# Masked attention over 64 keys against one-hot fetching of six picked keys, in a three-stage perceiver block

## The reference

```
xn   = layernorm(x) * gamma + beta
h    = xn @ W1.T                                     # 128 features
pair = relu(h[i] - h[j] + b1); pair = relu(pair @ W2.T + b2)
sim  = pair @ W3.T + b3;  sim[i, i] = 0              # 64 x 64 numbers
top6 = the six largest of each row of sim            # int(64 * 0.1) = 6
q, k, v = split(xn @ Wqkv.T + bqkv)                  # 32 heads of 2 features
scores  = q . k / sqrt(2), -inf where j is not in top6
out     = softmax(scores) @ v @ Wout.T + bout;  x + out
```

## Time and profile before

| | us |
|---|---|
| median of three runs | 2090.74 (2090.61 to 2090.97) |
| the profiled execution | 2089.24 |
| its span, first to last instruction | 2087.9 |

### The profile page before, as it was taken

The page is one execution under the profiler, slowest core; times in us unless marked ns, Lnnn a source line. Parts: engine busy times, 40 slices in busy tenths (PEclk is TensorE's granted clock), DMA queues, the critical chain, the costliest instruction groups (busy, mean ns, idle before and its releaser), DMA issues. The chain is left out here.

```text
span 2087.9 us, 31319 instructions
## 1 busy us (share of the span) xinstructions
PE 1943.7 (93%) x10316; PEld 1638.9 (78%) x10316; DVE 1152.3 (55%) x2987; ACT 968.3 (46%) x1955; POOL 649.3 (31%) x738
## 2 busy tenths in 40 slices
PE   3999999999999999999999999999999998758869
PEld 3778888888888888888888888888888887532447
DVE  6565465545554554466546655664556445148743
ACT  4564454446555654455445544554445444118221
POOL 3224543222232232333333333334333321011310
PEclk9999999999999999999999999999999999879769
DMA  5675454434453544354435444544444343720020
GB/s 191 207 258 158 118 151 121 150 106 148 141 182 116 162 136 137 115 168 144 133 106 168 144 142 123 177 143 153 119 155 144 96 145 92 250 81 3 1 81 20
DMA packets 228080, 280.94 MB, mean 135 GB/s; under 512 B 63241, under 2 KB 133513, under 8 KB 227921
## 3 DMA queue, kind: packets, MB, share of 16 engines
q1 hardware_dynamic: 217424, 278.09, 42.5%
q10 hardware_dynamic: 8448, 0.43, 0.2%
q0 software_dynamic: 2048, 0.43, 0.1%
HBM read 239.10 MB, written 39.22 MB: 133 GB/s over the span
## 5 line engine op out<-in xcount | busy, mean ns | idle before, releaser
L505 PE MATMUL kx_ps<-ctxT_hi,wk_hi 128*128 128x400 f32 (+1 forms) x1024 | 367.1, 358 | 16.0 <-DVE ctxT_lo L295 14.7
L507 PE MATMUL kx_ps<-ctxT_lo,wk_hi 128*128 128x400 f32 (+1 forms) x1024 | 356.9, 349 | 0.0
L509 PE MATMUL kx_ps<-ctxT_hi,wk_lo 128*128 128x400 f32 (+1 forms) x1024 | 356.2, 348 | 0.0
L588 PE MATMUL u_ps<-ctxN_hi,pt_hi 128*128 128x512 f32 (+1 forms) x832 | 341.5, 410 | 6.7 <-DVE pt_lo L826 6.4
L589 PE MATMUL u_ps<-ctxN_lo,pt_hi 128*128 128x512 f32 (+1 forms) x832 | 330.9, 398 | 0.0
L590 PE MATMUL u_ps<-ctxN_hi,pt_lo 128*128 128x512 f32 (+1 forms) x832 | 329.1, 396 | 0.0
L826 DVE TENSOR_TENSOR pt_lo<-t_ps,pt_hi 128x512 fp32r<-128x512 f32 (+1 forms) x256 | 144.6, 586 | 250.6 <-ACT pt_hi L1106 250.6
L1075 ACT ACTIVATE kx_hi<-kx_ps 128x400 fp32r<-128x400 f32 (+1 forms) x256 | 128.8, 503 | 320.6 <-PE kx_ps L509 317.3
L1106 ACT ACTIVATE pt_hi<-t_ps 128x512 fp32r<-128x512 f32 (+1 forms) x256 | 125.5, 523 | 265.1 <-PE t_ps L573 265.1
L753 DVE TENSOR_TENSOR kx_lo<-kx_ps,kx_hi 128x400 fp32r<-128x400 f32 (+1 forms) x256 | 146.6, 573 | 184.1 <-ACT sq L1077 183.5
L808 DVE CUSTOM_DVE_ANT_0 prob<-sc_ps,rstd_bc 128x400 f32<-128x400 f32 (+2 forms) x256 | 136.4, 570 | 140.1 <-PE sc_ps L561 140.1
(11 more groups left out here) (253 smaller groups left out, 3643.1 us busy)
## 6 DMA issues: line engine op xcount, KB each, us to landing
rstd_bc<-scratch_rstd SPq DMA_DIRECT2D x64, 804.0 KB, 6.0
stage<-in_ctx_t SPq DMA_DIRECT2D x96, 267.0 KB, 4.2
stage<-in_ctx_n SPq DMA_DIRECT2D x96, 256.0 KB, 6.1
wk_hi<-scratch_wk_s SPq DMA_DIRECT2D x56, 256.0 KB, 3.2
wk_lo<-scratch_wk_s SPq DMA_DIRECT2D x56, 256.0 KB, 3.7
wv_hi<-scratch_wv_s SPq DMA_DIRECT2D x56, 256.0 KB, 4.9
wv_lo<-scratch_wv_s SPq DMA_DIRECT2D x56, 256.0 KB, 5.6
scratch_own_rows<-out_sb SPq DMA_DIRECT2D x32, 256.0 KB, 2.9
```

The costliest lines, as they stand in the source:

```text
L505: PE.matmul(kx_ps[:, j % 2, 0:w], wk_hi[:, g % 2, i, :], ctxT_hi[:, i, c0:c0 + w], start=(i == 0), stop=False)
L507: PE.matmul(kx_ps[:, j % 2, 0:w], wk_hi[:, g % 2, i, :], ctxT_lo[:, i, c0:c0 + w], start=False, stop=False)
L509: mm = PE.matmul(kx_ps[:, j % 2, 0:w], wk_lo[:, g % 2, i, :], ctxT_hi[:, i, c0:c0 + w], start=False, stop=(i == C - 1))
L588: PE.matmul(u_ps[:], pt_hi[0:w, t % 2, cols], ctxN_hi[0:w, y, :], start=(y == 0), stop=False)
```

## The change

Only stage 2 and its loads are changed. In place of all 64 scores, only the six picked keys are computed. DVE writes a 0/1 mask laid out by batch (`mask`, 128 x 4 x 128). PE turns it, and one product with a triangular matrix (`rankmat`) numbers the picked keys of each token 1 to 6 (unpicked ones get a number that no rank matches). For each rank t, DVE makes a one-hot matrix (`hot`) and PE multiplies it with keys and values side by side (`kv`), which fetches key and value of rank t for every token and head. The rest works on 6 x 128 numbers for each partition, where x = 4 pairs of batches x 32 heads.

The query, key and value products become one product of 192 columns for each 128 tokens, with the bias as a product with a row of ones, and stand behind the pair loop in PE's order. The doubling of yT, the value blocks, the key spreads and the masks go. Tail.load has 7 counted DMAs in place of 11; the projection weights come in one DMA with rows of 768 bytes.

```diff
@@ Tail.load
-        for h in range(2):
-            SP.dma_start(self.wq2[:, :, h, :], qkv[:, :, 0:64]).then_inc(d_in, 16)
-        for h in range(2):
-            SP.dma_start(self.wk2[:, :, h, :], qkv[:, :, 64:128]).then_inc(d_in, 16)
-        SP.dma_start(self.wv[:], qkv[:, :, 128:192]).then_inc(d_in, 16)
+        SP.dma_start(self.wqkv[:], dram["wqkvT"].rearrange("(c p) o -> p c o", p=P)).then_inc(d_in, 16)
+        SP.dma_start(self.bqkv[0:1, :], dram["bqkv"]).then_inc(d_in, 16)
...
-        SP.dma_start(self.blockmask[:], dram["blockmask"]).then_inc(d_in, 16)
-        SP.dma_start(self.halfmask[:], dram["halfmask"]).then_inc(d_in, 16)
+        SP.dma_start(self.rankmat[:], dram["rankmat"]).then_inc(d_in, 16)
@@ tensor(), behind the h product: the products L1787, L1791, L1797 go
@@ tensor(), behind the pair loop: weigh and mix go, and
+            PE.wait_ge(zeroed, 4)
+            for t in range(4):
+                out = s_ps[:, 1 + t // 2, 192 * (t % 2):192 * (t % 2) + 192]
+                for c in range(4):
+                    PE.matmul(out, yT[:, c, t * P:(t + 1) * P], wqkv[:, c, :], start=(c == 0), stop=False)
+                mm = PE.matmul(out, one_row[0:1, :], bqkv[0:1, :], start=False, stop=True)
+                if t % 2:
+                    mm.then_inc(qkv_done, 1)
+            PE.wait_ge(topk_step, 12)
+            PE.wait_ge(sim_moved, 8)
             for k in range(4):
+                mm = PE.transpose(sim_ps[:, k * P:(k + 1) * P], mask[:, k, :], ident[:])
+            mm.then_inc(mask_turned, 1)
+            PE.wait_ge(mask_moved, 1)
+            PE.wait_ge(w3_set, 3)
+            PE.matmul(v_ps[:], rankmat[:], maskT[:], start=True, stop=True).then_inc(ranked, 1)
...
+            for t in range(TOPK):
+                PE.wait_ge(hot_done, t + 1)
+                for k in range(4):
+                    mm = PE.matmul(gather_banks[t][:, k * P:(k + 1) * P], hot[:, t, k * P:(k + 1) * P], kv[:, k, :],
+                                   start=True, stop=True)
+                mm.then_inc(gathered, 1)
@@ vector(): the copies L1871, the value blocks L1888 and L1891, and weigh and mix go, and
+            for b2 in range(2):
+                hr = slice(64 * b2, 64 * b2 + 64)
+                V.tensor_scalar(mask[hr, :, hr], picked[hr, :, 0:64], BIG, 1.0, ALU.is_equal, ALU.mult).then_inc(topk_step, 1)
+            def one_hot(t):
+                V.tensor_scalar(hot[:, t, :], v_ps[:], t - 99.0, 1.0, ALU.is_equal, ALU.mult).then_inc(hot_done, 1)
+            def multiply(t):
+                V.wait_ge(gathered, t + 1)
+                V.tensor_tensor(prod[:, t, :, :], gather_banks[t].rearrange("p (x f) -> p x f", f=4)[:, :, 0:2],
+                                q_sb[:].rearrange("p k (h d) -> p (k h) d", d=2), ALU.mult).then_inc(multiplied, 1)
+            V.wait_ge(ranked, 1)
+            V.wait_ge(qkv_moved, 4)
+            one_hot(0)
+            one_hot(1)
+            for t in range(TOPK):
+                if t + 2 < TOPK:
+                    one_hot(t + 2)
+                multiply(t)
+            V.wait_ge(multiplied, TOPK)
+            V.tensor_tensor(sc[:], prod[:, :, :, 0], prod[:, :, :, 1], ALU.add).then_inc(s_step, 1)
+            V.wait_ge(s_step, 1)
+            V.tensor_reduce(mx[:], sc[:].rearrange("p t x -> p x t"), AX.X, ALU.max).then_inc(s_step, 1)
+            V.wait_ge(s_step, 2)
+            V.tensor_tensor(sc[:], sc[:], mx[:].unsqueeze(1).broadcast_to([P, TOPK, P]), ALU.subtract).then_inc(s_step, 1)
+            V.wait_ge(s_exp, 1)
+            V.tensor_tensor(prod[:, 0:4, :, :].rearrange("p t x d -> p (t x) d"),
+                            s_ps[:].rearrange("p t (x f) -> p (t x) f", f=4)[:, :, 2:4],
+                            prob[:, 0:4, :].rearrange("p t x -> p (t x)").unsqueeze(2).broadcast_to([P, 4 * P, 2]),
+                            ALU.mult).then_inc(s_step, 1)
+            V.tensor_tensor(prod[:, 4:6, :, :].rearrange("p t x d -> p (t x) d"),
+                            b_ps[:].rearrange("p t (x f) -> p (t x) f", f=4)[:, :, 2:4],
+                            prob[:, 4:6, :].rearrange("p t x -> p (t x)").unsqueeze(2).broadcast_to([P, 2 * P, 2]),
+                            ALU.mult).then_inc(s_step, 1)
+            V.tensor_reduce(sm[:], prob[:].rearrange("p t x -> p x t"), AX.X, ALU.add).then_inc(s_step, 1)
+            V.wait_ge(s_step, 6)
+            V.reciprocal(inv[:], sm[:]).then_inc(s_step, 1)
+            V.tensor_reduce(mixed_sb[:], prod[:].rearrange("p t x d -> p x d t"), AX.X, ALU.add).then_inc(s_step, 1)
+            V.wait_ge(s_step, 8)
+            V.tensor_tensor(ao[:].rearrange("p k (h d) -> p (k h) d", d=2), mixed_sb[:],
+                            inv[:].unsqueeze(2).broadcast_to([P, P, 2]), ALU.mult).then_inc(ao_done, 1)
@@ scalar(): behind hT and hTb, in place of the query and key moves
+            A.wait_ge(zeroed, 1)
             for b2 in range(2):
                 hr = slice(64 * b2, 64 * b2 + 64)
+                A.activation(w3b[hr, b2:b2 + 1], core.col("w3")[hr, :], ACTF.Copy).then_inc(w3_set, 1)
+            A.activation(rankmat[:], tail.rankmat[:], ACTF.Copy).then_inc(w3_set, 1)
@@ scalar(): behind the pair loop, in place of the exponentials and moves
+            for pair in range(2):
+                A.wait_ge(qkv_done, pair + 1)
+                src = s_ps[:, 1 + pair, 0:384].rearrange("p (k e) -> p k e", k=2)
+                A.activation(kv[:, 2 * pair:2 * pair + 2, :], src[:, :, 64:192], ACTF.Copy).then_inc(qkv_moved, 1)
+                A.activation(q_sb[:, 2 * pair:2 * pair + 2, :], src[:, :, 0:64], ACTF.Copy).then_inc(qkv_moved, 1)
+            A.wait_ge(mask_turned, 1)
+            A.activation(maskT[:], sim_ps[:], ACTF.Copy).then_inc(mask_moved, 1)
+            A.wait_ge(s_step, 3)
+            A.activation(prob[:], sc[:], ACTF.Exp, scale=2.0 ** -0.5).then_inc(s_exp, 1)
@@ gpsimd(): the four key spreads L2018 go; four memsets stand ahead of the additions L2028 and L2031
+            G.memset(mask[:], 0.0).then_inc(zeroed, 1)
+            G.memset(one_row[:], 1.0).then_inc(zeroed, 1)
```

More of the change, by code:

```diff
@@ L27 @@
 N_ROWS = 0
-for _name, _n in (("bout", 512), ("ffn_b2", 512), ("bv", 64), ("wq_scale", 1), ("wqx_scale", 1),
+for _name, _n in (("bout", 512), ("ffn_b2", 512), ("wq_scale", 1), ("wqx_scale", 1),
                   ("wk_scale", 1), ("wv_scale", 1), ("proj_w_scale", 1), ("proj_in_scale", 1), ("b3", 1)):
@@ L1763, in sparse_attention @@
+        maskT, hot = sb("maskT", [P, 512], F32R), sb("hot", [P, TOPK, 512])
+        prod = sb("prod_d", [P, TOPK, P, 2])
+        sc, prob = sb("sc_d", [P, TOPK, P]), sb("prob_d", [P, TOPK, P])
+        mx, sm, inv = sb("mx_d", [P, P]), sb("sm_d", [P, P]), sb("inv_d", [P, P])
+        mixed_sb, ao, aoT = sb("mixed_d", [P, P, 2]), sb("ao_d", [P, 4, 64]), sb("aoT_d", [64, 512])
         banks = [b_ps[:, 0, :], b_ps[:, 1, :]]
         d_in = tail.d_in
-        hqk_done, v_done, doubled = sem("hqk_done"), sem("v_done"), sem("y_doubled")
@@ L1784, in tensor @@
                 mm = PE.matmul(s_ps[:, 0, :], wh[:, c, :], yT[:, c, :], start=(c == 0), stop=(c == 3))
-            mm.then_inc(hqk_done, 1)
-            for c in range(4):
-                mm = PE.matmul(s_ps[:, 1, :], wq2[:, c, :, :].rearrange("p h e -> p (h e)"), yT[:, c, :],
-                               start=(c == 0), stop=(c == 3))
-            mm.then_inc(hqk_done, 1)
-            for c in range(4):
-                mm = PE.matmul(s_ps[:, 2, :], wk2[:, c, :, :].rearrange("p h e -> p (h e)"), yT[:, c, :],
-                               start=(c == 0), stop=(c == 3))
-            mm.then_inc(hqk_done, 1)
-            PE.wait_ge(doubled, 2)
-            for b in range(8):
-                for c in range(4):
-                    mm = PE.matmul(v_ps[:, b * 64:(b + 1) * 64], vx_in[:, c, b, :, :].rearrange("p h s -> p (h s)"),
-                                   wv[:, c, :], start=(c == 0), stop=(c == 3))
-            mm.then_inc(v_done, 1)
+            mm.then_inc(h_done, 1)
             def last_layer(group):
@@ L1867, in vector @@
         def vector():
-            V.wait_ge(d_in, 16 * 11)
-            V.wait_ge(feat.moved, 8)
-            for h in range(2):
-                V.tensor_copy(vx_in[:, :, :, h, :], yT[:].rearrange("p c (b s) -> p c b s", b=8)).then_inc(doubled, 1)
             def first_layer(unit):
@@ L1913, in vector @@
             V.wait_ge(topk_step, 10)
-            V.tensor_scalar(mask[:], picked[:, :, 0:64], BIG, -1.0e30, ALU.not_equal, ALU.mult).then_inc(topk_step, 1)
-            V.wait_ge(topk_step, 11)
-            def weigh(k):
-                V.wait_ge(s_done, k + 1)
-                after(V, s_less, k)
-                V.scalar_tensor_tensor(sc[:], s_ps[:].rearrange("p i (h j) -> p (i h) j", j=64), 2.0 ** -0.5,
-                                       mask[:, k, :].unsqueeze(1).broadcast_to([P, 32, 64]), ALU.mult,
-                                       ALU.add).then_inc(s_masked, 1)
```

(43 more changed lines are left out.)

125 lines of the change are left out of this document (33 added, 92 removed).

## The result

The changed kernel takes a median of 2040.06 us (2038.77 to 2042.04, four runs) beside 2090.68 us (2089.38 to 2090.97) for the one before: a ratio of 0.976, 95% interval 0.9743 to 0.9777. The prediction was 2038.7, with a range of 2034.5 to 2046.5.

What follows compares the result with a forecast made beforehand. Attention was taken as a chain of engine hand-overs with no engine full, the pair loop as filled by DVE. Savings 6.0 + 8.4 + 37.6 = 52.0 off 2089.24, plus 1.5 for the median, gave 2038.7 us, range 2034.5 to 2046.5.

Steps and rivals of the forecast that it cites:

- Part A: End of stage 1: fewer, larger loads let projection block 4's weights arrive sooner, saving 6.0 us, ends 1.2 and 6.7.
- Part B: Start of the pair loop: DVE reaches the first even item sooner, shifting the loop by 8.4 us, ends 6.5 and 8.5.
- Part C: Masked attention: from the loop's last product to `ao` takes 25.5 us in place of 63.1, saving 37.6 us.
- a reduce above 1.5 us: Sign in the attention's DVE work that the forecast is wrong; the right sign was every 768-number reduce near 0.95 us.
- 0.7 us of the gap left: PE's wait ahead of projection block 4, 5.08 us before, shrinks to 0.7 us with the weights landing near 1791.
- one of 192 columns 0.46 x 192 / 512 = 0.17; 40 give 6.7: PE's query, key and value products behind the loop: 40 records at 0.17 us each, 6.7 us in all.
- I take the rate of the neighbouring ones.: Attention's DVE operations that step through memory priced as for neighbouring numbers: reduces of 768 at 0.95 us, of 1536 at 1.75.
- Rival 3: Stepping operands cost double on DVE in the attention: 6912 numbers, 7.2 us more, giving 2045.9 us; chance 7%.
- Rival 1: Block 4's weights stay late because DMA engines set the landing: 1.2 us gained in place of 6.0, 2043.5 us; chance 12%.
- Rival 2: PE at half clock in the attention's gathers: 2.8 to 5.7 us more, 2041.5 to 2044.4 us; chance 15%.
- Rival 4: PE stays at half clock through the pair loop and bounds it: 31 us longer, 2070 us; chance 4%.
- Rival 5: Stepping operands in DVE's chain behind the gathers so slow that nothing is gained: 68 us more, 2107 us; chance 2%.

Runs made afterwards that it cites:

- run 3: Changed kernel with the query, key and value weights loaded as before the change, in five DMAs of 64 columns, two into a spare tile: median 2047.35 us.
- run 2: Changed kernel with only the weights of projection block 4 issued ahead of the loads of stage 2: median 2038.21 us.
- run 8: Changed kernel with one-hot matrices, keys and values stored in fp32r, so each gather product is one pass: 2045.06 us, one run.
- Run 6: Changed kernel with all query, key and value products ahead of the pair loop and ACT's moves ahead of its first relu: median 2042.14 us.
- run 7: Changed kernel without the bias of queries, keys and values (four products left out): 2037.49 us, one run.
- run 4: Changed kernel with the six ranks side by side in products, scores and probabilities, so reduces read neighbouring numbers: median 2039.73 us.
- run 5: Changed kernel with the query, key and value products of two token blocks ahead of the pair loop, two behind it: median 2037.98 us.
- run 10: Changed kernel with two token blocks' products ahead of the pair loop, and two unread products filling PE's wait for the mask: 2040.23 us, one run.
- run 11: Changed kernel with one token block's products ahead of the loop, block 4's weights ahead of stage 2's loads, and ranks side by side: median 2036.74 us.
- run 12: The kernel of run 9 measured again, without an edit: median 2039.80 us.
- run 9: Changed kernel with one token block's query, key and value products ahead of the pair loop, three behind it: median 2038.18 us.

## Why the prediction was right, and where it was off

**The sum.** 52.0 was forecast and 48.2 came between the spans. From the parts: A 5.04, B 8.47, C 34.83 make 48.3, 3.7 less than forecast; the mechanisms held, and two sizes, in A and in C, were too large. Between the medians the difference is 50.6, so that only 1.4 us are left to the forecast of 2038.7. That closeness is luck: the profiled execution of the changed kernel was its slowest (2042.04, which is 2.3 above its span where the kernel before had 1.3), and the parts alone would put the median near 2042.4 (2090.7 - 48.3), still inside the range. Two of the prediction's own signs went against it: `ao` came 28.3 us from the end of the loop and not within 24 to 28, and the two reduces of 768 numbers took 1.45 and 1.43 us and not near 0.95 (its sign "a reduce above 1.5 us" was set badly, since its own sum had 1.75 for the last one).

The four rows of the table that the change doesn't touch (+2.93, -0.86, -1.59, -0.36) nearly cancel. The first lies inside the scatter of stage 1. The two in the middle follow the clock. In the stretch from the barrier up to the first difference (-1.59), the turns and the h product ran at 0.50 and then 0.75 to 0.80 in the kernel before and in run 3, and at 0.68 and then 1.00 in the changed kernel, where the h product took 3.67 us in place of 5.15:

```profile
1859.30:1865.00 5.70, 4.53 (x17) 3.51 (x18) 0.66 (x1) 3.11 (x4) 0.85 (x3) 0.50 0.76 254
...
1865.00:1870.80 5.80, 5.80 (x12) 2.48 (x11) 1.73 (x3) 1.17 (x2) 0.00 (x0) 0.80 1.05 397
```
```profile
1856.30:1862.00 5.70, 4.50 (x18) 3.48 (x19) 0.00 (x0) 3.02 (x4) 5.58 (x6) 0.68 0.79 258
...
1862.00:1866.20 4.20, 2.91 (x7) 0.95 (x5) 0.00 (x0) 1.19 (x3) 4.20 (x1) 1.00 1.05 400
```

The stretch took 11.5 to 11.8 us in runs 2, 3 and 8 as in the kernel before, and 9.9 to 10.1 in all others, so code that has the change shows both, and I don't count this gain to it.

**Part A, 6.0 forecast, 5.04 came**, inside its ends of 1.2 and 6.7. The mechanism is shown by run 3 (50.61 again) and run 2. The term that was off is the gap left, "0.7 us of the gap left": 1.53. "What the one new weight load stalls I take as one of the old ones, 2.5 us" was right at 2.46, and though the one-row bias load behind it stalled for another 2.52, SP came to block 4's weights 5.9 us sooner (9.1 us from x_c in place of 15.0), the forecast's "some 6 us". What was off is the landing: it followed the issue by 1794.47 - 1785.08 = 9.4 us, where it had been 7.15. Why it took longer no run shows. That the clock would hold across a short gap was right (first record 0.47, block 4 in 7.5).

**Part B, 8.4 forecast, 8.47 came.** The steps held: ACT close behind DVE, PE at half clock in the first items without effect. POOL's two additions took 4.5 us each and not 3.6; they were done at 1866.4, 0.2 us into the first difference instead of ahead of it, without a mark on it (six differences in 6.95 us, 6.90 before). Run 6 shows that the order of products and moves is worth 3.3 of it; the other 5.1 rest on the timeline.

**Part C, 37.6 forecast, 34.8 came**, the part with the real error. Two terms:
- "one of 192 columns 0.46 x 192 / 512 = 0.17; 40 give 6.7". The 0.17 was right for the records of 192 columns with 128 rows of weights (32 in 5.47 us, run 7); the eight bias records, of one row each, were priced as the others and add 0.33 each, 2.7 us in place of 1.4. +1.25 us, carried unchanged to the first one-hot (10.5 from the end of the loop, not 9.3) and to the last multiply (16.75, not 15.5). No row of the kernel before has a record with one row of weights.
- "I take the rate of the neighbouring ones." The three reduces that step 512 bytes and more took 5.52 us in place of 3.65, and run 4 shows that the step does it. The reciprocal gave 0.25 back (0.95 for 1.2).

The prediction weighed a rule of the Trainium skill here (Advanced Engine Details and Errata, Memory Cachelines, SBUF Cachelines): accesses that each go to another 16-byte line of SBUF pay a penalty. These runs agree with it: a step of 8 bytes cost nothing (0.96 us for 768), steps of 24 bytes in a write (0.60 for 0.42) and of 512 in a read (1.45 for 0.95) cost 0.6 to 0.75 ns more for each number. No run has single numbers 16 bytes apart in SBUF; the pairs 16 bytes apart are in PSUM. Rival 3 came in part: only 3072 of its 6912 numbers pay, 1.9 us and not 7.2.

**Rival 1** came in by a fifth: 0.96 of its 4.8 us. **Rival 2** did not come in the measured kernel but in seven of the twelve runs (5, 6, 7, 8, 10, 11, 12). Where one kernel has both (runs 9 and 12) it costs 1.65 us and not 2.8 to 5.7: the clock came back within four ranks (5.44 us in place of 3.81). That the measured kernel escaped it was in part luck: with this order of PE it came in one profile of six (run 8), and with PE's products moved or cut in six of seven. **Rival 4** did not come: the loop took 46.31. **Rival 5** did not come: the steps cost 0.6 to 0.75 ns for a number, where it needed 7.5.
